# Swin block on one core: the transposed tokens of attention as rounded part and remainder, Q, K and V as three rounded products each

## The reference

```python
h = _ln(x, g1, b1); h = roll(h, (-3, -3)); xw = win_part(h)      # windows of 7x7 = 49 tokens
q, k, v = split(xw @ w_qkv + b_qkv)                               # 4 heads of 32
attn = (q * HD ** -0.5) @ k.T + bias[rel_table] + MASK
out = softmax(attn) @ v
x = x + roll_back(win_rev(out @ w_proj + b_proj))
h2 = _ln(x, g2, b2)
return x + gelu(h2 @ w_fc1 + b_fc1) @ w_fc2 + b_fc2               # 128 -> 512 -> 128
```

## Time and profile before

| | us |
|---|---|
| median of 3 runs (lowest, highest) | 3276.6 (3276.32, 3279.51) |
| the profiled execution | 3275.45 |
| its span, first to last instruction | 3273.7 |
| PE busy | 3117.6 (95%) |
| DVE busy | 2814.3 (86%) |
| ACT busy | 2283.0 (70%) |
| POOL busy | 1316.7 (40%) |

### The profile page before, as it was taken

The page is one execution under the profiler, slowest core; times in us unless marked ns, Lnnn a source line. Parts: engine busy times, 40 slices in busy tenths (PEclk is TensorE's granted clock), DMA queues, the critical chain, the costliest instruction groups (busy, mean ns, idle before and its releaser), DMA issues.

```text
span 3273.7 us, 121784 instructions
## 1 busy us (share of the span) xinstructions
PE 3117.6 (95%) x51984; PEld 2750.4 (84%) x51984; DVE 2814.3 (86%) x7463; ACT 2283.0 (70%) x4478; POOL 1316.7 (40%) x775
## 2 busy tenths in 40 slices
PE   5999999999999999999999999999999999999998
PEld 4888888888888888888888888888888888888887
DVE  6888888888888888888888888888888888888885
ACT  3667766776777677767776777677767776776675
POOL 2344434443444444344434443444344434443442
PEclk9999999999999999999999999999999999999999
DMA  1111111111111111111111111111111111111110
GB/s 51 34 32 37 36 33 32 37 37 32 32 36 37 32 34 35 37 32 36 33 37 32 36 32 37 32 37 32 37 32 37 34 35 32 37 34 34 32 27 22
DMA packets 217584, 111.95 MB, mean 34 GB/s; under 512 B 15094, under 2 KB 216790, under 8 KB 217046
## 3 DMA queue, kind: packets, MB, share of 16 engines
q1 hardware_dynamic: 216899, 104.14, 12.4%
q10 hardware_dynamic: 147, 0.02, 0.0%
HBM read 52.73 MB, written 51.38 MB: 32 GB/s over the span
## 4 chain that ended last, share of the span: by engine, by line
DVE 43%; ACT 30%; PE 16%; issue 10%; SPq 0%; POOL 0%; DMA 0%; DVEq 0%; POOLq 0%; ACTq 0%
DVE stream L620 9%; DVE scores L600 8%; DVE row_max L603 8%; ACT hT L460 7%; DVE xn L588 6%; DVE raw L566 5%; ACT L482 5%; ACT qd L444 4%; PE psum L771 4%; ACT probsT L406 4%; PE psum L729 4%; DVE row_sum L613 4%; PE psum L773 3%; PE psum L772 3%; ACT xT L425 2%
## 5 line engine op out<-in xcount | busy, mean ns | idle before, releaser
L858 PE MATMUL psum<-wfc,hT 128*112 128x128 f32 x7168 | 835.6, 274 | 1.0 <-ACT hT L460 0.7
L858 PEld LDWEIGHTS psum<-wfc,hT 128*112 128x112 f32 x7168 | 797.8, 177 | 8.3 <-ACT hT L460 1.0
L356 POOL TENSOR_TENSOR probs<-probs,row_inv 128x784 f32<-128x784 f32 x256 | 389.4, 1521 | 987.1 <-DVE row_inv L615 987.1
L460 ACT ACTIVATE hT<-psum,bias_h 128x392 f32<-128x392 f32 x1024 | 598.8, 605 | 71.1 <-PE psum L773 70.7
L406 ACT ACTIVATE probsT<-psum 128x512 f32<-128x512 f32 x512 | 281.5, 613 | 484.7 <-PE psum L745 484.7
L588 DVE TENSOR_SCALAR xn<-x_in,mean,rstd 112x128 f32<-112x128 f32 x896 | 466.0, 587 | 1.8 <-POOL rstd L376 1.7
L368 POOL TENSOR_TENSOR stream<-stream,brow_fc 112x896 f32<-112x896 f32 x128 | 267.3, 2088 | 485.6 <-DVE xn L588 485.6
L771 PE MATMUL psum<-x2T_hi,wfc_hi 128*128 128x392 f32 x1024 | 448.7, 438 | 2.6 <-DVE x2T_lo L638 1.5
L400 ACT ACTIVATE probs<-scores 128x784 f32<-128x784 f32 x256 | 224.0, 875 | 210.0 <-DVE scores L605 210.0
L444 ACT ACTIVATE qd<-psum,bias_q,parity_one 128x392 f32<-128x392 f32 x512 | 318.4, 674 | 59.0 <-PE psum L773 55.8
L773 PE MATMUL psum<-x2T_lo,wfc_hi 128*128 128x392 f32 x1024 | 348.5, 340 | 0.0
(11 more groups left out here) (78 smaller groups left out, 5869.6 us busy)
## 6 DMA issues: line engine op xcount, KB each, us to landing
x_in<-in_x SPq DMA_DIRECT2D x224, 168.0 KB
out<-stream SPq DMA_DIRECT2D x224, 168.0 KB
x_in<-in_x SPq DMA_DIRECT2D x224, 17.5 KB
out<-stream SPq DMA_DIRECT2D x224, 17.5 KB
x_in<-in_x SPq DMA_DIRECT2D x224, 10.5 KB
out<-stream SPq DMA_DIRECT2D x224, 10.5 KB
x_in<-in_x SPq DMA_DIRECT2D x32, 96.0 KB
out<-stream SPq DMA_DIRECT2D x32, 96.0 KB
```

The costliest lines, as they stand in the source:

```text
L356: pool.tensor_tensor(p, p, r.unsqueeze(2).to_broadcast([128, 2 * WINDOWS, N]), ALU.mult).then_inc(probs_normed, 1)
L460: act.activation(hT[:, chunk, band * BAND:(band + 1) * BAND], tok_psum(FC1 + n)[:, 0:BAND], ACT.Gelu, bias=bias_h[:, chunk:chunk + 1]).the ...
L858: last = pe.matmul(tok_psum(FC2 + h)[0:TOK, (t - t0) * C:(t - t0 + 1) * C], hT[:, chunk, t * TOK:(t + 1) * TOK], wfc2[:, chunk, :], start= ...
```

## The change

`xT` is gone. ACT writes the rounded `xT_hi` for both bands straight from PSUM, and DVE writes `xT_lo` from PSUM minus `xT_hi`; both are double buffered in the 64-column layout. Q and K of both bands use the three rounded products, over 50 columns of each window. V uses three rounded products too. The weights of V are split once at the start. Probabilities are transposed as 113 rows instead of 128. Several steps stand elsewhere in the orders of POOL, ACT, DVE and PE. `round_x` is gone. The diff, cut to its core:

```diff
@@ tiles
-        xT = sb("xT", [C, 2, BANDS, WINDOWS, HALF])
-        xT_hi = sb("xT_hi", [C, BAND], F32R)
-        xT_lo = sb("xT_lo", [C, BAND], F32R)
+        xT_hi = sb("xT_hi", [C, 2, BANDS, WINDOWS, HALF], F32R)
+        xT_lo = sb("xT_lo", [C, 2, BANDS, WINDOWS, HALF], F32R)
+        wv_hi = sb("wv_hi", [C, C], F32R)
+        wv_lo = sb("wv_lo", [C, C], F32R)
@@ helpers (EVEN = 50)
+        def qk_psum(use):
+            return qkvo_psum(use)[:, 0:WINDOWS * EVEN].rearrange("c (w n) -> c w n", n=EVEN)[:, :, 0:N]
+        def x_windows(to, at, band, h):
+            t0, t1 = HALVES[h]
+            return to[:, at.slot(1) % 2, band, :, 0:N].rearrange("c w (i j) -> c w i j", j=WIN)[:, :, t0:t1, :]
+        def x_rows(band, h):
+            t0, t1 = HALVES[h]
+            rows = tok_psum(XT + h)[:, 0:(t1 - t0) * TOK].rearrange("c (t b w j) -> c w t b j", b=BANDS, w=WINDOWS, j=WIN)
+            return rows[:, :, :, band, :]
@@ POOL, step: the block that makes the next step's stream is now first instead of last
+                if at.has(1):
+                    wait(pool, x_loaded[at.slot(1)], dma_count(at.slot(1), at.image(1)))
...
+                                       ALU.add).then_inc(x_biased, 1)
                 if at.has():
                     normalise_probs(at, 0)
@@ ACT
             def copy_probsT(at, band):
+                rows = HALF + N
...
-                    act.activation(probsT[:, band, f, :, :, :].rearrange("p a q n -> p (a q n)"),
-                                   psum[:, S_BANK + 2 * band + f, :], ACT.Copy).then_inc(probsT_copied, 1)
+                    act.activation(probsT[:, band, f, :, :, :].rearrange("p a q n -> p a (q n)")[:, :, 0:rows],
+                                   psum[:, S_BANK + 2 * band + f, :].rearrange("p (a n) -> p a n", a=PAIRS)[:, :, 0:rows],
+                                   ACT.Copy).then_inc(probsT_copied, 1)
             def copy_x(at, h):
...
+                    last = act.activation(x_windows(xT_hi, at, band, h), x_rows(band, h), ACT.Copy)
                 last.then_inc(xT_copied, 1)
@@ ACT, step
                     copy_o(at, 0)
+                if at.has(1):
+                    copy_x(at, 1)
                 if at.has(-1):
                     copy_x2(at, 0)
-                if at.has(1):
-                    copy_x(at, 1)
...
-                if at.has(1):
-                    round_x(at)
@@ DVE
+            def split_x(at, h):
+                wait(dve, xT_copied, at.count(2, h + 1, 1))
+                for band in range(BANDS):
+                    last = dve.tensor_tensor(x_windows(xT_lo, at, band, h), x_rows(band, h),
+                                             x_windows(xT_hi, at, band, h), ALU.subtract)
+                last.then_inc(xT_split, 1)
@@ DVE, step
                     add_mlp(at, 0)
+                    add_mlp(at, 1)
                 if at.has(-1):
                     wait(dve, rstd2_ready, at.count(1, 1, -1))
                     wait(dve, x2T_made, at.count(2, 2, -2))
-                    normalise(xn2, stream[:, at.slot(-1), :, :], mean2, rstd2, xn2_ready)
-                if at.has(-2):
-                    add_mlp(at, 1)
-                if at.has():
+                    normalise(xn2, stream[:, at.slot(-1), :, :], mean2, rstd2, xn2_ready, 0)
+                if at.has(1):
+                    split_x(at, 0)
+                if at.has(-1):
+                    normalise(xn2, stream[:, at.slot(-1), :, :], mean2, rstd2, xn2_ready, 1)
+                if at.has(1):
+                    split_x(at, 1)
+                if at.has(-1):
+                    split_x2(at, 0)
+                if at.has():
+                    copy_v1(at)
                     inverse_sums(at, 1)
-                if at.has(-1):
-                    split_x2(at, 0)
-                if at.has():
-                    copy_v1(at)
                 if at.has(-1):
                     split_x2(at, 1)
...
-                if at.has(1):
-                    split_x(at)
@@ PE
             def transpose_probs(at, band):
+                rows = HALF + N
...
-                        last = pe.transpose(psum[:, S_BANK + 2 * band + f, 128 * pair:128 * (pair + 1)],
-                                            probs[:, band, f, 2 * pair:2 * pair + 2, :].rearrange("p w m -> p (w m)"),
-                                            ident[:, :])
+                        last = pe.transpose(psum[:, S_BANK + 2 * band + f, 128 * pair:128 * pair + rows],
+                                            probs[0:rows, band, f, 2 * pair:2 * pair + 2, :].rearrange("p w m -> p (w m)"),
+                                            ident[0:rows, 0:rows])
             def qk_product(at, use, part, band):
...
+                return product(qkvo_psum(use)[:, 0:WINDOWS * EVEN], wqk_hi[:, part, :], wqk_lo[:, part, :],
+                               xT_hi[:, at.slot(1) % 2, band, :, 0:EVEN], xT_lo[:, at.slot(1) % 2, band, :, 0:EVEN])
             def make_q(at, band):
+                wait(pe, xT_split, at.count(2, 2, 1))
                 wait(pe, o_copied, at.count(2, band + 1))
+                if band == 1:
+                    wait(pe, qk_copied, at.count(4, 2, 1))
@@ PE, make_values
-                rows = HALF + N
+                rows = HALF + EVEN
...
+                    pe.matmul(made, hi, wv_hi[:, :], start=True, stop=False)
+                    pe.matmul(made, hi, wv_lo[:, :], start=False, stop=False)
+                    last = pe.matmul(made, lo, wv_hi[:, :], start=False, stop=True)
@@ PE, transpose_x2
-                    wait(pe, xT_copied, at.count(2, h + 1, 1))
+                    wait(pe, xT_split, at.count(2, h + 1, 1))
@@ PE, step
                     attend(at, 0)
+                if at.has(1):
+                    transpose_x(at, 1)
+                if at.has():
+                    make_values(at, 1)
                 if at.has(-1):
                     transpose_x2(at, 0)
-                if at.has(1):
-                    transpose_x(at, 1)
-                if at.has():
-                    make_values(at, 1)
-                if at.has(-1):
                     transpose_x2(at, 1)
```

More of the change, by code:

```diff
@@ L359, in step @@
             def step(at):
+                if at.has(1):
+                    wait(pool, x_loaded[at.slot(1)], dma_count(at.slot(1), at.image(1)))
+                    wait(pool, xn1_ready, at.count(2, 2, 1))
+                    if at.has(1 - STEPS):
+                        wait(pool, out_stored[at.slot(1)], dma_count(at.slot(1), at.image(1 - STEPS)))
+                    pool.tensor_tensor(stream[:, at.slot(1), :, :], x_in[:, at.slot(1), :, :],
+                                       brow_proj[:, :].unsqueeze(1).to_broadcast([TOK, TILES, C]),
+                                       ALU.add).then_inc(x_biased, 1)
                 if at.has():
@@ L418, in copy_x @@
             def copy_x(at, h):
-                t0, t1 = HALVES[h]
                 wait(act, xT_made, at.count(2, h + 1, 1))
                 for band in range(BANDS):
[L423 to L426, removed]
+                    last = act.activation(x_windows(xT_hi, at, band, h), x_rows(band, h), ACT.Copy)
                 last.then_inc(xT_copied, 1)
[L429 to L433, removed]
             def copy_x2(at, h):
@@ L443, in copy_q @@
                 for parity in range(2):
-                    last = act.activation(qd[:, band, parity, :], qkvo_psum(Q_USE[band])[:, 0:BAND], ACT.Identity,
+                    last = act.activation(qd[:, band, parity, :].rearrange("c (w n) -> c w n", n=N), qk_psum(Q_USE[band]), ACT.Identity,
                                           bias=bias_q[:, parity:parity + 1], scale=parity_one[:, parity:parity + 1])
@@ L449, in copy_k @@
                 wait(act, qk_made, at.count(4, 2 * band + 2, 1))
-                act.activation(kT[:, band, :], qkvo_psum(K_USE[band])[:, 0:BAND], ACT.Identity,
+                act.activation(kT[:, band, :].rearrange("c (w n) -> c w n", n=N), qk_psum(K_USE[band]), ACT.Identity,
                                bias=bias_k[:, :]).then_inc(qk_copied, 1)
@@ L522, in _ @@
             dve.memset(probs[:, :, :, :, :], 0.0)
-            dve.memset(xT[:, :, :, :, :].rearrange("c s b w n -> c (s b w) n"), 0.0)
+            dve.memset(pad_zero[:, :], 0.0).then_inc(pad_zeroed, 1)
+            dve.wait_ge(pad_zeroed, 1)
+            for part in (xT_hi, xT_lo):
+                pad = part[:, :, :, :, N:HALF].rearrange("c s b w n -> c (s b w) n")
+                dve.tensor_copy(pad, pad_zero[:, :].unsqueeze(1).to_broadcast([C, 2 * BANDS * WINDOWS, HALF - N]))
             dve.memset(psum[:, 0:4, :], 0.0).then_inc(weights_ready, 1)
@@ L583, in mean_var, with normalise @@
                                          ALU.add).then_inc(ready, 1)
[L585 to L590, removed]
+            def normalise(dst, src, mean, rstd, ready, h):
+                for t in range(*HALVES[h]):
```

(29 more changed lines are left out.)

21 lines of the change are left out of this document (6 added, 15 removed).

## The result

| | before | changed |
|---|---|---|
| median us (lowest, highest) | 3278.06 (3276.32, 3280.09), 4 runs | 3469.05 (3468.35, 3469.76), 4 runs |
| span of the profiled execution | 3273.7 | 3467.9 |

The changed kernel takes 1.0582 times as long (95% interval 1.0564 to 1.0601): 191 us more. The forecast was 3474 us.

The account below looks back on a forecast made before the run. PE, with hardly any slack, was taken to be paced by results of DVE and ACT. +1.55 us a step times 128 = +198 us, plus 0.5 at the start, on 3275.45 gave 3474 us, range 3370 to 3600.

Parts of the forecast that it names:

- DVE's order: Second half of the step: DVE's new order delays `split_x2` and the sums of band 1; step 1.5 us longer.
- The walk: Clock times followed through DVE, PE, ACT and POOL from `add_mlp` 1 to Q of band 1; step 1.5 us longer.
- The two waits: PE before hidden 1 and before band 1's transposed probabilities: about 1.1 and 0.5 us, where one of 0.6 stood.
- V: V on PE, 12 rounded matmuls a band at 0.104 us instead of 8: 1.25 us, +0.38 per band.
- Rival 1: V on PE: narrow rounded matmuls no quicker than fp32, 2.6 us a band, step +4.3 us, 3826 us; chance 0.13.
- Q and K: Q and K on PE: band 0 gains 0.24 us, band 1's 8 extra columns cost 0.02; net -0.22 us a step.
- The sum: Whole step: 1.5 us plus 0.1 for V of band 0, given as +1.55 us, times 128 = +198 us.
- rival 2: ACT's lead and PE's later gaps absorb all but 0.3 to 0.7 us of lateness: 3315 to 3365 us; chance 0.06.
- rival 3: PE's own work decides, V 0.7 us, 0.32 us wait gone: -1.1 us a step, 3139 us; chance 0.05.
- Costed at nothing: `split_x` on DVE, L384's move on POOL, `xn1` 1.8 us shorter, earlier x loads, some new waits: no time on the path.

Follow-up runs that it names:

- the two moves: Changed kernel with sums of band 1 ahead of `split_x2` 0 and V of band 1 behind the first half of `transpose_x2`: 3307.69 us, ratio 1.0088.
- late sums alone: Kernel before, with only the sums of band 1 on DVE moved behind `split_x2` 0 and `copy_v1`: 3314.19 us, ratio 1.0108.
- L384 alone: Kernel before, with only POOL's L384 (the next step's stream) moved to the head of POOL's step: 3278.51 us, ratio 1.0001.
- The single moves: Changed kernel: sums earlier 3383.1, V of band 1 later 3399.09 us. Kernel before: end-of-step order 3219.93, `add_mlp` 1 earlier 3232.8, 113 rows 3266.22 us.

## Why the prediction was right, point by point

- **DVE's order, the main term.** The walk had the sums of band 1 about 3.3 us late, hidden 1 at 19.4, the transposes at 20.5, Q of band 1 at 24.3, and the step +1.55 us. The trace has +3.57, 19.41, 20.65, 24.18 and +1.44. The two waits were put at 1.1 and 0.5 us; they are 1.03 and 0.76 us of idle loads. The walk missed a third: it had hidden 0 only 0.5 us later and without a wait, while its load comes 1.04 us later, after 0.51 us of idle loads. The runs with the two moves show that this is the cause, and not only that it coincides.
- **V.** Taken: 0.104 us a matmul, between 0.06 and 0.218. Measured: 0.10 (1614.97 to 1615.07), so 1.2 us a band. Rival 1, that a narrow rounded matmul is no quicker than an fp32 one, is refuted: it would have shown 0.2. But V is still dearer in three rounded products (12 times 0.10 us) than in fp32 (8 times 0.109). Its 128 moving columns would take 0.06 us at the pace of 392 columns in 0.18 us, so what sets the distance is more likely the load: the first two loads of a product with 128 loaded columns are 0.11 us apart, and these with 114 are 0.10. Ten pairs take 1.00 us:

```profile
1614.97 0.26 PE L823 MATMUL psum<-wv_lo,xT_hi 128*114 128x128 f32 x1
...
1615.97 0.27 PE L824 MATMUL psum<-wv_hi,xT_lo 128*114 128x128 f32 x1
```

  The Trainium skill (TensorE: Matmul & The Clock Gate, section LDWEIGHTS) gives a load as its columns divided by 1.2 GHz, 95 ns for 114; the trace has 5 ns more. The 81 ns of the same page's section Back-to-back issue gap are not reached here, and the measurement decides.
- **Q and K, mis-sized.** I took 0.181 us for a rounded matmul of 400 columns. The trace has 0.19:

```profile
1617.23 0.36 PE L787 MATMUL psum<-xT_hi,wqk_lo 128*128 128x400 f32 x1
...
1617.42 0.35 PE L788 MATMUL psum<-xT_lo,wqk_hi 128*128 128x400 f32 x1
```

  With 0.57 us a product, band 0 gains 0.18 and band 1 loses 0.07, so this part of PE's work is -0.11 us a step and not -0.22. Of it only band 1's 0.07 us stands behind the last wait and so in the step's time: from Q of band 1 to the next step are 2.39 us, where I had 2.3 as before. The same timeline has 392 columns at 0.18. Whether 8 more columns or the gaps of 14 in the new layout cost it was not tried.
- **The sum.** I added 0.1 us for V of band 0 in the first half; the trace shows 0.01. The walk had Q of band 1 1.49 us later; measured 1.37. These two were too large, and the 0.07 us behind Q was missing. The addition itself has a slip: 1.49 and 0.1 make 1.6, not 1.55, which is 6 us more over 128 steps.
- **Luck in the number.** The mechanism was right, but an error of 5 us flatters it. The step was put 0.11 us too long, 14 us over the run. Against that stand 0.5 us for the start of the program, where both ends of the run cost 7 us, and a base 2.6 us below the median of 3278.06 us that was measured for the kernel before.
- **Absorbed lateness, rival 2.** It is present, but smaller than the rival had it: of 2.1 us at the transposes 1.4 are left at Q of band 1. The kernel with late sums alone shows the mechanism (ACT's queue is the later one), and there I over-sized the loss almost threefold.
- **Faster, rival 3.** Its condition, sums less than 1.0 us later, was not met. What it was built on, 1.8 us less on DVE, did come and was worth nothing, as L384 alone shows.
- **Costed at nothing.** `split_x` is hidden: its four instructions take 0.68 and 0.56 us a pair, and DVE waits after them for `copy_x2` 0, 0.69 us in this step. Once V stands behind `transpose_x2`, `split_x` is hidden no more, as that run shows. L384 brings no wait at its new place; it runs from 1625.82 to 1627.94, while DVE waits for the next scores, and not beside the maximum and the bias addition, as I had it.

```profile
L649 DVE TENSOR_TENSOR x2T_lo<-psum,x2T_hi 128x448 fp32r<-128x448 f32 (+1 forms) x256 | 137.0, 535 | 90.9 <-ACT x2T_hi L446 90.9
```

## What to carry to other kernels

Where each engine's order is written out by hand, an edit that adds an operation also sets what stands behind it: write down for each result who waits for it and how much slack it has, and put the results with none (here `split_x2` and the sums) first. Time taken off an engine counts only if it comes ahead of a result on which the path waits; 1.8 us a step behind the last such result were worth nothing. And when a change is slower, reorder before giving up on it: the same instructions gave 3469 and 3213 us.

## What was not expected

The single moves add up almost exactly in this kernel (86 + 70 against 161, 58 + 45 + 11 against 115), although each of them shifts the waits of all later work. And a wait of some 0.3 us in the profile, PE for `copy_o` ahead of Q of band 1, was worth 58 us, 0.45 us a step. The wait of 0.23 us is only what the profile calls idle. From the last matmul before Q to Q's first are 0.56 us, where 0.18 us is the usual distance, and from Q's first to its second 0.26 us: 0.38 and 0.08 us more than without the wait.
